# Two of four expert outputs by accumulating scatter into a DRAM table, in a gated cross-attention and mixture-of-experts kernel

## What is computed

```python
E, K, CAP = 64, 6, 64                                  # experts, choices per token, slots per expert
scores = softmax(xf @ gate_w.T)
topk_w, topk_idx = top_k(scores, K)
# buf_tok[e, c]: the tokens of expert e, T where a slot is empty; buf_w: their scores
gx  = xp[buf_tok]                                      # (64, 64, 256)
g, u = split(einsum('ech,ehi->eci', gx, gate_up_proj), 2)
eo  = einsum('eci,eih->ech', silu(g) * u, down_proj) * buf_w[..., None]
routed = zeros((T + 1, h)).at[buf_tok.reshape(-1)].add(eo.reshape(-1, h))[:T]
shared = silu(xf @ shared_gate_w.T) * (xf @ shared_up_w.T) @ shared_down_w.T
out = x + tanh(g_ffn) * (routed + shared)
```

## Time and profile before

| | us |
|---|---|
| runs | 796.70, 798.79, 799.75 |
| median | 798.79 |
| the profiled execution | 796.67 |
| its span in the profile | 794.9 |
| of it, up to the first up product | 660.8 |
| from there to the end of the last combine | 128.2 |
| from there to the end of the span | 5.9 |

### The profile page before, as it was taken

One profiled execution on the slowest core, in us unless ns is written; L12 is line 12 of the kernel. 1 busy time (PEld: TensorE's weight loads), 2 busy tenths in 40 slices (PEclk: granted clock), 3 DMA queues, 4 the chain that ended last, 5 costly groups with the idle time before them and its releaser, 6 DMA issues.

```text
span 794.9 us, 15421 instructions
## 1 busy us (share of the span) xinstructions
PE 717.0 (90%) x4913; PEld 584.5 (74%) x4913; DVE 604.7 (76%) x1286; ACT 466.3 (59%) x1179; POOL 448.1 (56%) x585
## 2 busy tenths in 40 slices
PE   3748899899999989999998999998978799999996
PEld 3646787778888778888886878877856666777775
DVE  6867888788898869788887888888888783454444
ACT  5646867677686766768677676866655232222221
POOL 2425777566767756677776667776866315222220
PEclk9979999999999999999999999999999999999999
DMA  6310100100001010001001010000002015666661
GB/s 186 113 54 1 33 23 1 54 28 28 1 27 29 1 54 28 27 1 28 28 2 52 3 34 2 27 1 2 1 1 61 21 48 148 192 194 190 189 186 54
DMA packets 44479, 42.76 MB, mean 54 GB/s; under 512 B 3717, under 2 KB 43386, under 8 KB 44410
## 3 DMA queue, kind: packets, MB, share of 16 engines
q1 hardware_dynamic: 41706, 36.61, 15.1%
q0 software_dynamic: 1536, 5.28, 2.5%
q10 hardware_dynamic: 1168, 0.01, 0.1%
HBM read 39.52 MB, written 2.37 MB: 53 GB/s over the span
## 4 chain that ended last, share of the span: by engine, by line
PE 63%; DVE 18%; ACT 7%; issue 6%; POOL 4%; ACTq 1%; DMA 0%; POOLq 0%; DVEq 0%
PE out_ps L1760 8%; PE s_ps L1531 7%; PE proj_ps L1487 6%; PE pT_ps L1540 6%; PE proj_ps L1472 6%; PE aux_ps L1550 5%; PE aux_ps L1564 5%; DVE q_tok L1103 5%; PE aux_ps L1501 4%; PE proj_ps L1463 4%; POOL rstd L528 3%; PE work_ps L1752 3%; DVE ss L1083 2%; PE work_ps L1774 2%; PE aux_ps L1408 2%
## 5 line engine op out<-in xcount | busy, mean ns | idle before, releaser
L543 POOL TENSOR_SCALAR p_sb<-p_sb,psum_row 128x256 f32<-128x256 f32 x256 | 125.5, 507 | 67.6 <-DVE psum_row L1122 66.3
L798 ACT ACTIVATE p_sb<-s_ps,negmax 128x256 f32<-128x256 f32 x256 | 118.5, 473 | 64.0 <-DVE negmax L1117 62.8
L1550 PE MATMUL aux_ps<-pT_sb,v_sb 128*128 128x512 f32 x256 | 120.7, 593 | 4.0 <-DVE pT_sb L1128 4.0
L1531 PE MATMUL s_ps<-kT,qT 128*128 128x256 f32 x768 | 112.3, 289 | 8.2 <-DVE qT L1113 4.6
L1128 DVE COPY pT_sb<-pT_ps 128x512 f32<-128x512 f32 x128 | 87.6, 685 | 41.2 <-PE pT_ps L1540 40.5
L550 POOL TENSOR_TENSOR y_bf<-y_bf,mg_bf 128x512 bf16<-128x512 bf16 x64 | 85.9, 1342 | 58.4 <-DVE mg_bf L1140 58.3
L1531 PEld LDWEIGHTS s_ps<-kT,qT 128*128 128x128 f32 x768 | 97.6, 190 | 18.3 <-issue 18.3
L1117 DVE TENSOR_REDUCE negmax<-s_ps 128x2 f32<-128x512 f32 x128 | 86.4, 683 | 5.9 <-PE s_ps L1531 5.6
L528 POOL TENSOR_TENSOR rstd<-var,minus_half 128x8 f32<-128x8 f32 (+1 forms) x64 | 85.7, 1339 | 5.3
L553 POOL TENSOR_TENSOR catq<-y_bf,mg_bf 128x512 fp32r<-128x512 bf16 x64 | 79.6, 1243 | 5.0
L1564 PE MATMUL aux_ps<-wpT,catq 128*128 128x256 f32 x512 | 69.1, 288 | 5.9 <-DVE wkvT L1031 4.8
(11 more groups left out here) (188 smaller groups left out, 1394.9 us busy)
## 6 DMA issues: line engine op xcount, KB each, us to landing
w_up_a<-in_L_ffn_gate_up_proj SPq DMA_DIRECT2D x16, 384.0 KB, 3.5
w_up_b<-in_L_ffn_gate_up_proj SPq DMA_DIRECT2D x16, 384.0 KB, 3.6
wp_raw<-in_L_xattn_wproj SPq DMA_DIRECT2D x16, 256.0 KB, 2.9
w_down_a<-in_L_ffn_down_proj SPq DMA_DIRECT2D x16, 192.0 KB, 3.7
w_down_b<-in_L_ffn_down_proj SPq DMA_DIRECT2D x16, 192.0 KB, 3.6
w_raw<-in_L_xattn_w_kv_x SPq DMA_DIRECT2D x8, 256.0 KB, 4.6
w_raw<-in_L_xattn_wq SPq DMA_DIRECT2D x7, 256.0 KB, 2.7
w_raw<-in_L_xattn_wqx SPq DMA_DIRECT2D x7, 256.0 KB, 3.0
```

The costliest lines, as they stand in the source:

```text
L543: ins = nc.gpsimd.tensor_scalar(p_sb[:, r, st, :], p_sb[:, r, st, :], rsum[:, r, st:st + 1], 1.0, ALU.mult, ALU.mult)
L798: ins = nc.scalar.activation(p_sb[:, r, st, :], s_ps[:, r % 2, st, :], ACT.Exp, bias=negmax[:, r, st:st + 1], accum_out=psum_row[:, r, st: ...
L1531: ins = nc.tensor.matmul(s_ps[:, k % 2, st, :], qT[:, a, ty, h, st * P:(st + 1) * P], kT[:, b, ty, s.gi, :], start=(i == 0), stop=(i == 2))
L1550: ins = nc.tensor.matmul(aux_ps[:, f.bank, :], v_sb[:, (2 * s.n + tt) % VRING, ty, s.gi, :], pT_sb[:, ty, :, tt, :], start=(tt == 0), stop ...
```

## The change

Of each group of four pairs, pairs u = 0 and u = 2 (not in the last group) no longer go through the one-hot product. DVE scales the pair's output in one operation into `eo_whole` (`eo_all`), and POOL adds it to a DRAM table `sums_dram` of 1024 + 64 rows by two accumulating indirect DMAs, one for each expert of the pair (64 rows of 1 KB each). Empty slots add to 64 spare rows, each slot to its own. POOL waits for each scatter to land before it issues the next. The table is cleared beforehand by a store from SP, and at the end SP loads it (1 MB) and DVE adds it, times the gate, to x, in the last step, ahead of the last pair's low part. The other pairs go on as before; their counts come from `kept`.

The loop is also skewed by one more step. In step i PE does the hid transpose of i, up of i+1, the gather transposes of i+2, the combine of i-1 if that pair is kept (both parts together), and down of i. `w_slot` has four columns instead of two. POOL's two-half line of a group is: index copy, gathers 0 and 1, second index copy, the scatters of the group before with gathers 2 and 3 between them.

```diff
+        SCATTERED = (0, 2)
+        def scattered(u, kind):
+            return u in SCATTERED and kind != "last"
+        def kept(it, u, kind):
+            before = it * (RING - len(SCATTERED))
+            return before + (u if kind == "last" or u < 0 else sum(v not in SCATTERED for v in range(u)))
...
             sp.dma_start(rows_dram[T:T + 1, :], zero_row[:, :]).then_inc(rows_stored, 16)
+            sp.wait_ge(eo_clear, 1)
+            sp.dma_start(sums_dram[0:T, :].rearrange("(n p) h -> p n h", p=P),
+                         eo_whole[:, 0:1, :].to_broadcast([P, NT, H])).then_inc(sums_cleared, 16)
+            sp.dma_start(sums_dram[T:T + CAP, :], eo_whole[0:CAP, 0, :]).then_inc(sums_cleared, 16)
...
+            for k in range(2):
+                sp.wait_ge(sums_added[k], 32 * (NIT - 1))
+            sp.dma_start(sums_sb[:, :, :], sums_dram[0:T, :].rearrange("(n p) h -> p n h", p=P)).then_inc(sums_loaded, 16)
...
             nc.gpsimd.memset(zero_row[:, :], 0.0).then_inc(f_const_ready, 1)
+            nc.gpsimd.memset(eo_whole[:, :, :], 0.0).then_inc(eo_clear, 1)
+            nc.gpsimd.iota(slot_no[:, :], pattern=[[0, 1]], base=0, channel_multiplier=1,
...
+            def gather(it, u):
+                pool.wait_ge(gxT_filled, it * RING + (u - RING + 1))
+                pool.sem_inc(pool_turn, 1)
+                pool.wait_ge(w_slot_ready, it * RING + (u - RING + 1))
+                pool.sem_inc(pool_turn, 1)
+                nc.gpsimd.indirect_dma_start(gx[:, u, :], None, rows_dram[:, :],
+                                             bass.IndirectOffsetOnAxis(idx_cur[:, u:u + 1], 0)
+                                             ).then_inc(gx_loaded[u], 16)
+            def add_sums(it, k, e):
+                half = slice(e * CAP, (e + 1) * CAP)
+                nc.gpsimd.indirect_dma_start(sums_dram[:, :],
+                                             bass.IndirectOffsetOnAxis(idx_sums[:, e, SCATTERED[k]:SCATTERED[k] + 1], 0),
+                                             eo_whole[half, k, :], None, compute_op=ALU.add
+                                             ).then_inc(sums_added[k], 16)
+            def gathers_and_sums(it, first):
+                for u in range(RING):
+                    pool.wait_ge(gx_loaded[u], it * 16)
...
+                nc.gpsimd.tensor_copy(idx_cur[:, :], idx_all[:, bass.ds(it * RING, RING)]).then_inc(idx_copied, 1)
+                pool.wait_ge(idx_copied, it)
+                pool.sem_inc(pool_turn, 1)
+                gather(it, 0)
+                gather(it, 1)
...
+                    pool.wait_ge(sums_added[1], it * 32 - 32)
+                pool.sem_inc(pool_turn, 1)
+                nc.gpsimd.tensor_copy(idx_sums[:, :, :], idx_both[:, :, bass.ds(it * RING - RING, RING)]
+                                      ).then_inc(sums_idx, 1)
+                pool.wait_ge(sums_idx, it)
+                pool.sem_inc(pool_turn, 1)
+                pool.wait_ge(eo_ready, it * RING + (SCATTERED[0] - RING + 1))
+                pool.sem_inc(pool_turn, 1)
+                add_sums(it, 0, 0)
+                gather(it, 2)
+                pool.wait_ge(sums_added[0], it * 32 - 16)
+                pool.sem_inc(pool_turn, 1)
+                add_sums(it, 0, 1)
+                gather(it, 3)
+                pool.wait_ge(sums_added[0], it * 32)
+                pool.sem_inc(pool_turn, 1)
+                pool.wait_ge(eo_ready, it * RING + (SCATTERED[1] - RING + 1))
+                pool.sem_inc(pool_turn, 1)
+                add_sums(it, 1, 0)
+                pool.wait_ge(sums_added[1], it * 32 - 16)
+                pool.sem_inc(pool_turn, 1)
+                add_sums(it, 1, 1)
...
# ACT, pairs
+                    if not (kind == "last" and u == RING - 1):
+                        silus(i + 1)
+                    if not (kind == "last" and u >= RING - 2):
+                        evac_gxT(i + 2, u + 2)
+                    if not scattered(u, kind):
+                        eo_hi(it, u, kind)
...
# DVE
+            link(nc.vector.tensor_scalar(empty_row[:, :], work_ps[0:CAP, 0, 0:2 * NPAIR], float(T), slot_no[:, 0:1],
+                                         ALU.is_ge, ALU.mult))
+            nc.vector.tensor_tensor(idx_both[:, :, :].rearrange("p e n -> p (e n)"), work_ps[0:CAP, 0, 0:2 * NPAIR],
+                                    empty_row[:, :], ALU.add).then_inc(idx_ready, 1)
...
+            def eo_all(it, u):
+                k = SCATTERED.index(u)
+                dve.wait_ge(down_done, it * RING + (u + 1))
+                wait(dve, sums_added[k], it * 32)
+                dve.wait_ge(sums_cleared, 32)
+                nc.vector.tensor_scalar(eo_whole[:, k, :], work_ps[:, 3, 0:H], w_slot[:, u:u + 1], 1.0,
+                                        ALU.mult, ALU.mult).then_inc(eo_ready, 1)
+            def add_scattered(n):
+                nc.vector.scalar_tensor_tensor(x_sb[:, n, :], sums_sb[:, n, :], gate[:, 2:3], x_sb[:, n, :],
+                                               ALU.mult, ALU.add).then_inc(scattered_in, 1)
...
+                for u in range(RING):
+                    i = it * RING + u
+                    if not (kind == "last" and u >= RING - 2):
+                        take_scores(it + (u + 2) // RING, i + 2, (u + 2) % RING)
+                    evac_hidT(i)
+                    if not (kind == "last" and u == RING - 1):
+                        gated(i + 1)
+                    if scattered(u, kind):
+                        eo_all(it, u)
+                    else:
+                        build_onehot(it, u, kind)
+                        if kind == "last" and u == RING - 1:
+                            dve.wait_ge(gate_ready, 2)
+                            dve.wait_ge(sums_loaded, 16)
+                            for n in range(NT):
+                                add_scattered(n)
+                        eo_lo(it, u, kind)
...
# PE
-            ins.then_inc(slots_done, 1)
+            nc.tensor.matmul(work_ps[0:CAP, 0, NPAIR:2 * NPAIR], tok[:, :], pick[:, 1, :], start=True, stop=True
+                             ).then_inc(slots_done, 1)
...
             def pairs(it, kind):
+                for u in range(RING):
+                    i = it * RING + u
+                    transpose_hid(i)
+                    if not (kind == "last" and u == RING - 1):
+                        up(it + (u + 1) // RING, i + 1, (u + 1) % RING)
+                    if not (kind == "last" and u >= RING - 2):
+                        transpose_gx(it + (u + 2) // RING, i + 2, (u + 2) % RING)
+                    if u == 0 and kind != "first":
+                        combine_pair(it - 1, RING - 1, "mid")
+                    elif u > 0 and not scattered(u - 1, kind):
+                        combine_pair(it, u - 1, kind)
+                    down(i, u)
```

More of the change, by code:

```diff
@@ L279, in flamingo_kernel @@
         eo_ready = sem("eo_ready")
+        eo_clear = sem("eo_clear")
+        slot_no_ready = sem("slot_no_ready")
+        sums_cleared = sem("sums_cleared")
+        sums_added = [sem(f"sums_added{k}") for k in range(2)]
+        sums_idx = sem("sums_idx")
+        sums_loaded = sem("sums_loaded")
+        scattered_in = sem("scattered_in")
         onehot_ready = sem("onehot_ready")
@@ L617, in _ @@
             pool.wait_ge(rows_stored, 32)
[L619 to L625, removed]
-                    pool.sem_inc(pool_turn, 1)
[L627 to L636, removed]
@@ L643, in _ @@
+            for u in range(RING):
+                nc.gpsimd.indirect_dma_start(gx[:, u, :], None, rows_dram[:, :],
+                                             bass.IndirectOffsetOnAxis(idx_all[:, u:u + 1], 0)
+                                             ).then_inc(gx_loaded[u], 16)
+            gathers_and_sums(1, True)
+            with pool.Fori(2, NIT) as it:
+                gathers_and_sums(it, False)
         @block.scalar
@@ L1359, in pairs @@
             def pairs(it, kind):
[L1360 to L1367, removed]
+                for u in range(RING):
+                    i = it * RING + u
+                    if not (kind == "last" and u >= RING - 2):
[5 more added lines that the diff above has]
+                        eo_all(it, u)
+                    else:
+                        build_onehot(it, u, kind)
[5 more added lines that the diff above has]
+                        eo_lo(it, u, kind)
+            take_scores(0, 0, 0)
+            take_scores(0, 1, 1)
+            gated(0)
             pairs(0, "first")
@@ L1776, in down, with combine_pair @@
                 ins.then_inc(down_done, 1)
-            def pairs(it, kind):
[L1779 to L1783, removed]
-                    if not prev:
-                        for k in range(8):
-                            nc.tensor.transpose(work_ps[:, 3, (k % 4) * P:(k % 4 + 1) * P], ident[:, :], ident[:, :])
-                    if prev:
-                        pe.wait_ge(eo_hi_ready, i)
```

(27 more changed lines are left out.)

57 lines of the change are left out of this document (30 added, 27 removed).

## The result

| | before | after |
|---|---|---|
| median of 4 runs, us | 797.91 | 833.84 |
| lowest to highest | 796.70 to 799.75 | 830.56 to 836.20 |
| the profiled execution | 796.67 | 836.20 |
| its span | 794.9 | 834.4 |
| final adds begin | 789.10 | 828.62 |

The change costs time: the ratio after to before is 1.0441, interval 1.0419 to 1.0462. The forecast was 793.8 us, with a range up to 812.

What follows compares the result with a forecast made beforehand. PE bounds the kernel now; POOL's line of chained scatters, 15.66 us a round, would replace it. Seven rounds, table load, adds and last half combine end at 784.1 against 789.1, 5.0 less: 793.8 us, range 777 to 812.

Steps and rivals of the forecast that it cites:

- POOL takes PE's place as the bound: Expert loop: POOL's line takes 15.66 us per four pairs, PE's work 11.7, so the 29.4 us removed are not gained.
- the return leg from the fourth scatter to the next round's first: POOL's line: issue, index copies, two gathers and gaps between these two scatter starts, 6.0 us.
- the skew: Expert loop: PE's, ScalarE's and DVE's work in another order, priced at nothing, under each round's 4 us of PE waiting.
- the preparation: Before the loop: clearing the table and small extra PE and DVE work are hidden, under 1 us if uncovered.
- the final adds wait for the table: Kernel's end: SP loads the 1 MB table until 779.2, PE being ready at 778.7; this wait would show the forecast right.
- The condition named for a loss: POOL's line: if a scatter's landing exceeds 2.65 us, the round exceeds 16.35 and the end passes 789.1.
- the one that prices the scatter: POOL's line: a 64-row scatter, absent from the trace, estimated from a gather's parts at 2.42 us, between 1.93 and 3.05.
- The issue: POOL's time to issue a 64-row scatter, between half and a whole gather's, 0.48 to 0.95; taken as 0.72 us.
- The landing, 2.42: Scatter from issue start to semaphore: 0.72 issue, 0.6, 0.6 data, 0.5; between 1.93 and 3.05 us.
- Busier, not the bound: DMA engines in the loop: 10 us for four pairs plus four times 0.6 to 1.0 for scatters, within 15.7 us.
- Rival 1: POOL's scatters land slowly, above 2.65 us, making the kernel slower than before; 808.9 us at 3.05; chance 0.33.
- its far price, 828 us: POOL's line with scatters landing as late as the slowest gather, 3.9 us: round 20.3 us, kernel 828 us.

Runs made afterwards that it cites:

- e1: Changed kernel with no pair scattered and the table neither loaded nor added, only the reordered loop: 796.56 us, ratio 0.9984 to the kernel before.
- e6: Changed kernel with one 128-row scatter per scattered pair into a table twice as long, 2 MB loaded and 16 tiles added: 787.87 us, ratio 0.9861 to before.
- e2: Changed kernel without expert weight loads after the first four pairs, whose weights all later pairs use: 813.90 us, ratio 1.0191 to before.
- e3: Changed kernel with scatters that overwrite rows instead of adding to them: 813.26 us, ratio 1.0183 to before.
- e4: Changed kernel with a separate table for each expert of a pair, the second not cleared, loaded or added: 795.19 us, ratio 0.9952 to before.
- e5: Changed kernel with only pair 0 of each four scattered, gathers 2 and 3 between its two scatters: 785.25 us, ratio 0.9824 to before.

## Why the prediction was wrong

**Right.** POOL takes PE's place as the bound, and PE waits for gathers; the return leg from the fourth scatter to the next round's first is 6.0 (6.13 measured); a scatter that waited begins 0.8 after the landing (700.35 to 701.15); the skew costs nothing (e1); the preparation costs under 1 us (0.55 at most); POOL does not wait for the scaled outputs (the view puts 7.7 us down to DVE, but the two long ones, 4.4 and 2.3 us, end 0.9 after a scatter's landing, at 685.16 and 788.45); the final adds wait for the table. The condition named for a loss, a landing above 2.65, is met.

**The step that failed is the one that prices the scatter** ("A scatter is no row of this trace"). Three choices in it:
- The issue was scaled by rows to 0.72. It is 1.42: rows hardly count (plain 64 rows 0.91, gather of 128 rows 0.95; adding 128 rows 1.62 in e6), and the add costs POOL 0.5. Even the upper end, 0.95, was too low, because it had no term for the add in the issue.
- The landing, 2.42, is a plain scatter's (2.3). The adding one takes 3.2 (median of e2) even when quiet, above 3.05, the upper end that I had worked out. I had leaned on a store and a load against a gather's 2.96; e3's plain scatter is indeed near these 2.1 and 2.2, but none of them adds, and the 0.8 between the shortest of each, 2.3 and 3.1, is the add (0.5 in the issue, 0.3 behind it).
- The meeting with the weight loads was left out. The scatter's parts were taken from a gather on an otherwise idle machine, and the sum has no term for company. Beside the loads scatters take 4.2 to 4.8, in the first round up to 6.3. "Busier, not the bound" is right for throughput (e4) and wrong for delay: in a chain of landings, delay is the bound.

The first two make most of the 15.4 that e2 keeps of the six rounds' 33.4 us, the third the other 18.0; the last round pays 5.0 more. Rival 1 had the mechanism; its far price, 828 us, has a landing of 3.9 but an issue of 0.95. The range, cut at 812, left its far part out, and the measured 833.84 lies beyond even that price. Its chance, 0.33, was too small: every indirect DMA of the trace (2.8 to 3.9) stood on its side, and two plain ones on mine.

The Trainium skill's page "DMA: Bandwidth & Descriptors" (Anatomy of one DMA — SWDGE (gpsimd) path) gives an estimated 2.15 us for 64 KB. The runs lie on both sides of it: behind the issue a plain scatter takes 1.4 and an adding one 1.7 when quiet, 2.8 to 3.35 beside the weight loads of the round above. Taken from issue to landing it is near the plain scatter's 2.3 and short of the adding one's 3.1, and that section prices neither the add nor the company. It pointed the right way, in part by luck: put behind my issue it made up for an issue that was too short.

**Not foreseen, and small.** The table took 5.6 us from the last landing to the start of its adds, instead of 4.3. The last half combine ran at the lower clock, after PE had stood (1.94 for 1.15). And 4.5 us of the profiled difference lie ahead of the loop, in the clock of unchanged work.

**Open.** How much of a late landing is due to the bursts of weight loads and how much to any load (e5 has a median of 4.6 under a steady share of 0.82) was not separated. The mean share alone does not tell it: from 700 to 780 it is 0.62 before and 0.63 after, and yet the slowest gather of the loop goes from 3.9 to 5.9 us (line L652 of after; 3.4 in e2). Also open are why the clock falls in an unchanged stage in some executions and not in others, and what holds e6's round.

## What to carry to other kernels

Before counting what comes off the bound engine, price the in-order queue that takes the work over: per chained DMA its issue, its landing under the load that it will meet there, and the wake-up, each for that kind of DMA. Then move only as much as keeps that line shorter than the bound: one pair of four gained 1.8%, two lost 4.4%. Where transfers wait for each other only because they may touch the same rows, give them different rows: separate tables took the round from 21.2 to 15.5 us with the same DMAs in flight, in a run that leaves the second table out of the result.

## What the runs showed of the hardware

- Issue on POOL: gather of 128 rows 0.95 us, plain scatter of 64 rows 0.91, adding scatter of 64 rows 1.42, of 128 rows 1.62.
- From issue to landing: plain scatter 2.3 (shortest and median of e3), adding scatter 3.1 to 3.2 without weight loads (e2), 4.2 to 4.8 beside them in the round shown, up to 6.3 over all.
- PE after 8 us of standing: 3.64 us, at a granted clock of 0.50, for a combine that takes 2.15 at 1.00 later in the same round.
- Executions of the unchanged kernel differ by up to 5.6 us: 796.45 at a mean granted clock of 0.990, 802.08 at 0.977.
